# Attention B: turned probabilities as one fp32 copy, and an fp32 product with fp32 values

## The reference

```
q = (resid @ Wq) in 32 heads of 16, with rotary embedding
k, v = (resid @ Wk), (resid @ Wv) in 8 heads of 16; k with rotary embedding
att = einsum('bhgqd,bhkd->bhgqk', q, k) / sqrt(16), causal mask
probs = softmax(att)
ctx = einsum('bhgqk,bhkd->bhgqd', probs, v)
out = ctx @ Wo
```

## Time and profile before

| | us |
|---|---|
| median of 3 runs | 1158.74 (1157.28 to 1158.85) |
| the profiled execution | 1155.95 |
| its span, first to last instruction | 1154.1 |
| mean PE clock granted, share of full | 0.982 |

### The profile page before, as it was taken

The page is one execution under the profiler, slowest core; times in us unless marked ns, Lnnn a source line. Parts: engine busy times, 40 slices in busy tenths (PEclk is TensorE's granted clock), DMA queues, the critical chain, the costliest instruction groups (busy, mean ns, idle before and its releaser), DMA issues.

```text
span 1154.1 us, 25383 instructions
## 1 busy us (share of the span) xinstructions
PE 1019.4 (88%) x8608; PEld 631.0 (55%) x8608; DVE 902.5 (78%) x2021; ACT 706.9 (61%) x1561; POOL 683.6 (59%) x808
## 2 busy tenths in 40 slices
PE   1688999999999999999999978798777777777898
PEld 1345555555555555555555534455466666666554
DVE  5777877877778877877778876787779999999755
ACT  2157666666656666656666553346778888888331
POOL 3678786777678767867776514465445555555211
PEclk9999999999999999999999999899989999999999
DMA  7065354735744753555566350000000000000001
GB/s 275 16 178 142 109 139 122 170 80 137 179 118 80 191 122 74 170 142 139 108 128 156 92 127 11 1 1 1 1 1 2 0 0 0 0 0 0 1 1 73
DMA packets 180268, 94.94 MB, mean 82 GB/s; under 512 B 168288, under 2 KB 169056, under 8 KB 175584
## 3 DMA queue, kind: packets, MB, share of 16 engines
q1 hardware_dynamic: 170832, 50.85, 20.8%
q10 hardware_dynamic: 9360, 43.01, 11.4%
HBM read 49.64 MB, written 2.26 MB: 45 GB/s over the span
## 4 chain that ended last, share of the span: by engine, by line
PE 70%; ACT 11%; DVE 7%; issue 5%; POOL 3%; DMA 2%; SPq 0%; ACTq 0%; DVEq 0%; POOLq 0%
PE bank L942 14%; PE bank L944 14%; PE bank L943 14%; ACT prob L705 5%; PE bank L1273 5%; ACT ptb_hi L712 3%; PE bank L1240 3%; PE bank L1023 3%; PE bank L1024 3%; PE bank L1025 3%; PE bank L1044 3%; PE bank L1046 3%; PE bank L1045 3%; DVE xn L1364 2%; PE bank L1026 1%
## 5 line engine op out<-in xcount | busy, mean ns | idle before, releaser
L478 POOL TENSOR_TENSOR rt<-rt 128x512 f32<-128x512 f32 x80 | 101.0, 1266 | 157.6 <-DVE rt L1441 157.6
L1488 DVE SCALAR_TENSOR_TENSOR bw_hi<-bank,rden,bw_hi 128x128 f16<-128x128 f32 (+3 forms) x256 | 123.3, 544 | 60.4 <-ACT bw_hi L722 60.4
L694 ACT ACTIVATE bank<-bank,shift,c_score 128x128 f32<-128x128 f32 (+3 forms) x256 | 147.1, 604 | 2.1
L705 ACT ACTIVATE prob<-bank,shift,c_score_b 128x128 f32<-128x128 f32 (+3 forms) x256 | 137.5, 632 | 0.0
L722 ACT ACTIVATE bw_hi<-bank,rden 128x128 f16<-128x128 f32 (+3 forms) x256 | 114.0, 529 | 32.8 <-DVE rden L1481 32.8
L1455 DVE TENSOR_REDUCE smax<-bank 128x1 f32<-128x512 f32 (+3 forms) x256 | 109.3, 484 | 26.1 <-PE bank L1026 24.6
L1465 DVE TENSOR_REDUCE smax<-bank 128x1 f32<-128x128 f32 (+3 forms) x256 | 113.4, 485 | 18.7 <-PE bank L1245 16.4
L1240 PE MATMUL bank<-kt_b,qt_b 128*128 (+4 forms) x256 | 72.1, 308 | 53.7 <-ACT prob L705 53.5
L689 ACT ACTIVATE shift<-smax,c_score 128x4 f32<-128x4 f32 x64 | 19.0, 297 | 158.9 <-DVE smax L1455 158.9
L634 POOL TENSOR_TENSOR shift<-smax,c_score_b 128x1 f32<-128x1 f32 (+1 forms) x192 | 36.6, 191 | 110.3 <-DVE smax L1465 101.8
L942 PE MATMUL bank<-xt_hi,wq_hi 128*128 128x512 f16 x256 | 98.4, 384 | 3.4 <-DVE rt L1441 2.2
(11 more groups left out here) (217 smaller groups left out, 3227.4 us busy)
## 6 DMA issues: line engine op xcount, KB each, us to landing
qcode<-in_q_codes ACTq DMA_DIRECT2D x8, 1024.0 KB, 4.9
qscale<-scales_q ACTq DMA_DIRECT2D x7, 1024.0 KB, 7.6
ocode<-in_o_codes ACTq DMA_DIRECT2D x7, 1024.0 KB, 5.0
oscale<-scales_o ACTq DMA_DIRECT2D x7, 1024.0 KB, 8.4
kvcode<-in_k_codes ACTq DMA_DIRECT2D x8, 256.0 KB, 7.9
kvcode<-in_v_codes ACTq DMA_DIRECT2D x8, 256.0 KB, 8.3
x<-in_x SPq DMA_DIRECT2D x2, 1024.0 KB, 7.1
out<-x SPq DMA_DIRECT2D x8, 256.0 KB, 2.0
```

The lines of the kernel that those rows point to most:

```text
L694: act.activation(a_rows(i, s), a_rows(i, s), ACT.Exp, bias=shift[:, s % 2, c:c + 1], scale=c_score[:, 0:1], accum_out=bank[3][:, SUMS_AT + ...
L705: act.activation(prob[:, i2, S_OFF[i]:S_OFF[i] + w], bank[bk][:, o:o + w], ACT.Exp, bias=shift[:, i2, c:c + 1], scale=score[:, 0:1]).then_ ...
L1488: dve.scalar_tensor_tensor(out=p_row[:, s % 2, LO_AT[i]:LO_AT[i] + P_STEP * i + 1:P_STEP], in0=turned_back(i, s), scalar=rden[:, s % 2, c: ...
```

## The change

The halves of the turned probabilities and of the values are replaced by one fp32 tile each, `ptb` and `bv`. ACT copies pieces 0 and 2 to `ptb`, DVE piece 1; the factor 2^15 is gone; POOL has no part in it any more. `b_pv` issues one fp32 matmul where `three` stood, ten in place of thirty. DVE's `bv_lo` is gone and ACT writes the values as fp32. Turning row tile 0 now waits for ACT's copies of the step before, where it waited for DVE.

```
@@ -262,8 +262,7 @@
-        bv_hi = sb("bv_hi", [P, NT, KV_HEADS * B_VD], F16)
-        bv_lo = sb("bv_lo", [P, NT, KV_HEADS * B_VD], F16)
+        bv = sb("bv", [P, NT, KV_HEADS * B_VD], F32)
@@ -298,9 +297,7 @@
-        ptb_hi = sb("ptb_hi", [P, 2, TRI], F16)
-        ptb_lo = sb("ptb_lo", [P, 2, TRI], F16)
-        ptb_32 = sb("ptb_32", [P, 2, TRI - 2 * S], F32)
+        ptb = sb("ptb", [P, 2, TRI], F32)
@@ -349,13 +346,12 @@
...
@@ -594,9 +590,8 @@
             pool.memset(kt_b[:].rearrange("p h f n -> p (h f n)").bitcast(F32), 0.0).then_inc(zeros_done, 1)
-            for v, value in ((bv_hi, 1.0), (bv_lo, 0.0)):
-                pool.memset(v[:].rearrange("p t (h d) -> p t h d", d=B_VD)[:, :, :, B_HD:B_VD], value
-                            ).then_inc(zeros_done, 1)
+            pool.memset(bv[:].rearrange("p t (h d) -> p t h d", d=B_VD)[:, :, :, B_HD:B_VD], 1.0
+                        ).then_inc(zeros_done, 1)
@@ -616,16 +611,6 @@
-            def b_last_piece(n, i2):
...
-                piece = slice(2 * S, TRI)
-                pool.wait_ge(bpt, 3 * n + 1)
-                pool.tensor_tensor(ptb_hi[:, i2, piece], ptb_32[:, i2],
-                                   one[:].broadcast_to([P, TRI - 2 * S]), ALU.mult).then_inc(bpthi_last, 1)
-                pool.wait_ge(bpthi_last, n + 1)
-                pool.tensor_tensor(ptb_lo[:, i2, piece], ptb_32[:, i2], ptb_hi[:, i2, piece], ALU.subtract
-                                   ).then_inc(bpt_last, 1)
@@ -633,13 +618,10 @@
                                            c_score_b[:, 1:2].broadcast_to([P, c1 - c0]), ALU.mult).then_inc(bshift, 1)
-                    if not (first and s == 0):
-                        b_last_piece(n - 1, (s - 1) % 2)
...
                 b_group(j, False)
-            b_last_piece(8 * KV_HEADS - 1, 1)
@@ -705,12 +687,12 @@
-            def pt_high(base, piece, ps, done, scale, pt, banks):
...
-                w = S if piece < 2 else 2 * P
-                act.wait_ge(ps, base + piece + 1)
-                act.activation(pt[:, piece * S:piece * S + w], bank[banks[piece]][:, 0:w], ACT.Copy,
-                               scale=scale).then_inc(done, 1)
+            def b_turned(n, i2, piece):
...
+                w = S if piece < 2 else TRI - 2 * S
+                act.wait_ge(bpt_ps, 3 * n + piece + 1)
+                act.activation(ptb[:, i2, piece * S:piece * S + w], bank[B_PT_BANK[i2][piece]][:, 0:w], ACT.Copy
+                               ).then_inc(bpt_act, 1)
@@ -876,8 +858,8 @@
                 act.wait_ge(bkv_ps, t + 1)
-                act.activation(heads_v(bv_hi, t), bank[5 + t % 2][:, P:2 * P].rearrange("p (h d) -> p h d", d=B_HD),
-                               ACT.Copy, scale=PROJ_DN_B).then_inc(bv_hi_done, 1)
+                act.activation(heads_v(bv, t), bank[5 + t % 2][:, P:2 * P].rearrange("p (h d) -> p h d", d=B_HD),
+                               ACT.Copy, scale=PROJ_DN_B).then_inc(bv_done, 1)
@@ -893,7 +875,7 @@
                 if t == 0:
-                    act.wait_ge(zeros_done, 3)
+                    act.wait_ge(zeros_done, 2)
@@ -920,16 +902,15 @@
                     if not (first and s == 0):
-                        for piece in range(2):
-                            pt_high(3 * (n - 1), piece, bpt_ps, bpthi, P_UP, ptb_hi[:, (s - 1) % 2],
-                                    B_PT_BANK[(s - 1) % 2])
+                        for piece in (0, 2):
+                            b_turned(n - 1, (s - 1) % 2, piece)
...
                 b_group(j, False)
-            for piece in range(2):
-                pt_high(3 * (8 * KV_HEADS - 1), piece, bpt_ps, bpthi, P_UP, ptb_hi[:, 1], B_PT_BANK[1])
+            for piece in (0, 2):
+                b_turned(8 * KV_HEADS - 1, 1, piece)
@@ -1219,7 +1200,7 @@
                 if t >= 2:
-                    pe.wait_ge(bv_lo_done, t - 1)
+                    pe.wait_ge(bv_done, t - 1)
@@ -1256,13 +1237,13 @@
             pe.wait_ge(bt_act, 3 * NT)
-            pe.wait_ge(bv_lo_done, NT)
+            pe.wait_ge(bv_done, NT)
...
                 if i == 0 and not first:
-                    pe.wait_ge(bpt, 3 * n - 1)
+                    pe.wait_ge(bpt_act, 2 * n)
@@ -1280,16 +1261,15 @@
                     pe.wait_ge(bctx, n)
-                pe.wait_ge(bpt, 3 * n + 3)
-                pe.wait_ge(bpt_last, n + 1)
+                pe.wait_ge(bpt_act, 2 * n + 2)
+                pe.wait_ge(bpt_dve, n + 1)
                 vc = bass.ds(j * B_VD, B_VD)
-                hi, lo = ptb_hi[:, s % 2], ptb_lo[:, s % 2]
...
                         tc = slice(T_OFF[kt] + (i - kt) * P, T_OFF[kt] + (i - kt + 1) * P)
-                        vh, vl = bv_hi[:, b * ST + kt, vc], bv_lo[:, b * ST + kt, vc]
-                        mm = three(o_ap, hi[:, tc], lo[:, tc], vh, vl, kt, i + 1)
+                        mm = pe.matmul(o_ap, ptb[:, s % 2, tc], bv[:, b * ST + kt, vc], start=(kt == 0),
+                                       stop=(kt == i))
@@ -1464,13 +1444,6 @@
-            def pt_low(count, piece, hi_done, done, scale, hi, lo, banks):
-                w = S if piece < 2 else 2 * P
-                c = slice(piece * S, piece * S + w)
-                dve.wait_ge(hi_done, count)
-                dve.scalar_tensor_tensor(out=lo[:, c], in0=bank[banks[piece]][:, 0:w], scalar=scale, in1=hi[:, c],
-                                         op0=ALU.mult, op1=ALU.subtract).then_inc(done, 1)
@@ -1735,11 +1708,6 @@
                                   ALU.subtract).then_inc(bk_lo, 1)
-                dve.wait_ge(bv_hi_done, t + 1)
-                dve.scalar_tensor_tensor(out=heads_v(bv_lo, t),
-                                         in0=bank[5 + t % 2][:, P:2 * P].rearrange("p (h d) -> p h d", d=B_HD),
-                                         scalar=PROJ_DN_B, in1=heads_v(bv_hi, t), op0=ALU.mult,
-                                         op1=ALU.subtract).then_inc(bv_lo_done, 1)
@@ -1791,17 +1759,10 @@
-            def b_low_piece(n, i2, piece):
-                pt_low(2 * n + piece + 1, piece, bpthi, bpt, P_UP, ptb_hi[:, i2], ptb_lo[:, i2], B_PT_BANK[i2])
...
-            def b_low(n, i2, first):
...
-                if not first:
-                    dve.wait_ge(bpt_last, n - 1)
-                dve.wait_ge(bpt_ps, 3 * n + 3)
-                dve.tensor_scalar(ptb_32[:, i2], bank[B_PT_BANK[i2][2]][:, 0:TRI - 2 * S], P_UP, None, ALU.mult
-                                  ).then_inc(bpt, 1)
-                b_low_piece(n, i2, 0)
+            def b_turned(n, i2):
...
+                dve.wait_ge(bpt_ps, 3 * n + 2)
+                dve.tensor_copy(ptb[:, i2, S:2 * S], bank[B_PT_BANK[i2][1]][:]).then_inc(bpt_dve, 1)
@@ -1810,11 +1771,9 @@
                     if not (first and s < 1):
-                        b_low(n - 1, (s - 1) % 2, first and s < 3)
+                        b_turned(n - 1, (s - 1) % 2)
...
                         b_rden(n - 2, s % 2, first and s < 4)
-                    if not (first and s < 1):
-                        b_low_piece(n - 1, (s - 1) % 2, 1)
@@ -1824,8 +1783,7 @@
             last = 8 * KV_HEADS - 1
-            b_low(last, 1, False)
-            b_low_piece(last, 1, 1)
+            b_turned(last, 1)
```

More of the change, by code:

```diff
@@ L350, in build @@
                              "mt_ps", "mthi_done", "mt_done", "y_ps", "y_added"))
-        bq_ps, bkv_ps, bq_mul, bk_mul, bq_rot, bk_rot, bq_hi, bk_hi, bv_hi_done, bq_lo, bk_lo, bv_lo_done = (
+        bq_ps, bkv_ps, bq_mul, bk_mul, bq_rot, bk_rot, bq_hi, bk_hi, bv_done, bq_lo, bk_lo = (
             sem(n) for n in ("bq_ps", "bkv_ps", "bq_mul", "bk_mul", "bq_rot", "bk_rot", "bq_hi", "bk_hi",
-                             "bv_hi_done", "bq_lo", "bk_lo", "bv_lo_done"))
+                             "bv_done", "bq_lo", "bk_lo"))
         zeros_done, bt_ps, bt_act, bt_dve = (sem(n) for n in ("zeros_done", "bt_ps", "bt_act", "bt_dve"))
-        bs_ps, bsmax, bshift, bexp, brden, bpt_ps, bpthi, bpt, bpthi_last, bpt_last, bctx_ps, bctx = (sem(n) for n in (
-            "bs_ps", "bsmax", "bshift", "bexp", "brden", "bpt_ps", "bpthi", "bpt",
-            "bpthi_last", "bpt_last", "bctx_ps", "bctx"))
+        bs_ps, bsmax, bshift, bexp, brden, bpt_ps, bpt_act, bpt_dve, bctx_ps, bctx = (sem(n) for n in (
+            "bs_ps", "bsmax", "bshift", "bexp", "brden", "bpt_ps", "bpt_act", "bpt_dve", "bctx_ps", "bctx"))
         def load_codes(eng, n, j):
```

## The result

The changed kernel takes 1186.13 us (median of 4 runs, 1185.4 to 1187.78) against 1158.45 us (1157.28 to 1158.85) for the kernel before on the same chip: ratio 1.0243, 95% interval 1.0225 to 1.026, or 27.7 us more where 13.8 less was forecast. The profiled execution took 1185.75 us, with a span of 1183.9. One of ten executions of the kernel with the old division of the pieces took 1556.65 us at a mean granted clock of 0.659, against 0.98 in the others, and is left out of its time.

A forecast was written before the change was run, and what follows sets the result against it. It took a loop of ACT and PE, 3.54 us a head, to bound the kernel. Steps -13.4, projections -1.4, first heads +1.0 and end 0 gave -13.8 us: 1144.9 us from 1158.74, range 1138 to 1200.

The forecast's parts named there:

- the term of PE's product: PE, `b_pv`: two pairs of load and matmul a product at 70 ns each, ten products 1.40 us.
- rival B: PE, `b_pv`: four pairs a product, 220 to 280 ns, step 4.09 to 4.69 us, about 1193 to 1230 us; chance 0.20.
- rival E: PE clock falls to the 1.2 GHz level: steps 4.6 us and more, 1220 us and up; chance 0.04.
- rival C: PE product: two pairs of 83 to 111 ns, load not overlapping the matmul before; 1158 to 1193 us; chance 0.10.
- Room on PE: PE, first product matmul to next scores: 1.65 us, or 1.43 with the shortened step, hiding products up to 143 ns each.
- ACT's copies: Attention B, ACT: 256 columns fewer save 0.22 us a step, 3.54 to 3.32; 61 steps give -13.4 us.
- DVE and POOL: Attention B: DVE loses 1.09 us a step, POOL two operations; neither in the chain, so worth nothing.
- Projections: `bv_lo` leaves DVE ahead of the rotary products: seven times 0.20, 1.4 us less.
- the ring: Projections: DVE's rotary products, POOL's sum, ACT's copies and DVE's norm wait for each other; if another arm takes over, nothing saved.
- First heads: First heads of attention B at low clock: PE paces, one product falls in at double price, +1.0 us.
- The end: Last product 0.65 us longer, a DVE L1472 ahead of the reciprocal gives 0.67; zero.

The follow-up runs named there:

- the old division of the pieces: Against the kernel with single fp16 values and one pass: ACT copies pieces 0 and 1, DVE piece 2; 1154.91 us, 0.9969 of the kernel before.
- runs with 17, 64 and 128 columns: Changed kernel itself (17 moving columns in each fp32 product), and widened to 64 or 128: 1186.13, 1185.79 and 1190.57 us.
- the run with turns made as products: Against the kernel with single fp16 values and one pass: transposes replaced by fp32 matmuls with the identity; 1208.7 us against 1140.03.
- runs with four, seven and ten products: Changed kernel with six or three of its ten fp32 products left out, or none: 1141.29, 1145.4 and 1186.13 us.
- one fp16 number: Changed kernel with turned probabilities and values kept as fp16, low halves left out, multiplied in one pass: 1140.03 us, 0.9854 of the kernel before.
- The mixed kernel: Against the kernel before: four products (piece 1) fp32, six as three fp16 passes, ACT copies piece 2 as fp32, POOL splits it; 1145.75 us, 0.9894.

## Why the prediction was wrong

**The step that failed is the term of PE's product**: "A pair costs the fp16 distance plus the longer load, 25 + 45 = 70 ns". The number of pairs, two a product, was right (1280 matmuls, 20 a head), which rules out rival B; the clock of 1.00 in the steady steps rules out rival E. The pair takes 110 ns. Ten products are 2.19 us, not 1.40, against a room of 1.43. The size is that of rival C, which I gave a chance of 0.10: 83 to 111 ns a pair, step up to 4.11, up to 1193 us; measured 4.08 and 1186.

C's reason did not come true with its size. It said that a load cannot overlap the short matmul before it. But matmuls of 128 columns leave the distance at 114 ns, so load and matmul do overlap. And the forecast's reason for two pairs (one matmul carries both parts of the moving number) is not shown by the right count.

Two errors made the 70. First, the price of a pair stood in the nearest row: the turns start 111 ns apart. I took that for 128 columns at two cycles each and expected 17 columns to be cheaper. The runs with 17, 64 and 128 columns have 110, 112 and 114 ns: the price does not shrink with the columns. Second, I built the price from the lengths of two load records, and a record's length is not its occupancy: a turn's load lasts 141 ns and a product's 192, yet both pairs start 110 to 111 ns apart. (That the kind of matmul makes the load's record longer, not the data, is shown by the run with turns made as products.) Where the trace has no such pair back to back, the honest price was the whole interval between 25 and 111 ns, which put the threshold of 71.5 ns a pair in its middle and not 1.5 ns beside the forecast.

**Room on PE.** Right. The formula 3.54 + 2.19 - 1.65 = 4.08 gives the measured step. The runs with four, seven and ten products lie below, at and above the threshold, at 3.42 (mean), 3.40 and 4.08 us.

**ACT's copies.** Right in mechanism and near in size, but covered up by PE: 377 ns for the 256 columns against 376 expected, and 0.19 to 0.20 us a step where the product leaves it free (four products, one fp16 number), against 0.22. The division of the pieces alone is worth 1.2% by the ratios, 13 to 14 us.

**DVE and POOL.** Right for the steady steps: worth nothing there by themselves (old division, 3.63 against 3.61 us). Not quite right for the first heads of the kernel before, where the chain has 1.6 us of DVE in it (row maximum, L1802 and L1472, in the chain before):

```profile
847.54 0.69 DVE smax L1465
848.23 0.33 DVE ptb L1802
848.56 0.61 DVE ptb_lo L1472
```

**Projections.** Half of the 1.4 us: from the first rotary product of the queries to the last lie 46.7 us before (779.8 to 826.5) and 46.0 after (780.0 to 826.0). The mixed kernel, with `bv_lo` back, has 46.9 again (780.2 to 827.1), so the half that came is that instruction's. The other half did not come; another arm of the ring probably takes over, which no run tests.

**First heads.** The sign was wrong. In the stretches shown with the result the clock is at full from 843 us on, where the kernel before has 0.50 of it until 847.5, in the first stretch below. No product falls into the low clock any more: the first one starts at 844.74 us, when the clock is already at full. So it is not the fp32 product that brings the clock up earlier. The other runs agree. The kernel with one fp16 number has no fp32 product and is at 1.00 from 843 us on; the mixed kernel has four a head and is at 0.50 until 847.5. What does bring it up is not shown; the two kernels with the late rise are those in which DVE and POOL still make halves. The lines are from the kernel before, the changed kernel (two), the one with one fp16 number and the mixed one.

```profile
835.00:847.50 12.50, 8.65 (x46) 6.10 (x45) 6.15 (x15) 8.76 (x17) 2.81 (x10) 0.50 0.00 1
```
```profile
842.20:844.60 2.40, 1.75 (x17) 1.60 (x18) 2.21 (x5) 1.98 (x5) 0.43 (x3) 1.00 0.00 0
```
```profile
844.74 0.68 PE L1271 MATMUL bank<-bv,ptb 128*128 128x17 f32 x5
```
```profile
843.00:851.00 8.00, 5.54 (x73) 4.65 (x71) 6.26 (x16) 6.99 (x16) 1.53 (x8) 1.00 0.00 0
```
```profile
835.00:847.50 12.50, 8.62 (x42) 6.27 (x43) 6.37 (x14) 8.37 (x16) 2.77 (x10) 0.50 0.00 0
```

The earlier rise is why it is +25.5 us between the first and the last exponential, and not 61 x 0.46 = 28 (0.46 is 4.07 less the mean of 3.61).

**The end.** Forecast zero, measured 4.9 us from the last exponential on. The forecast counted one product there. The chain now holds two, of heads 62 and 63:

```profile
1096.71 2.15 PE bank L1271 x20
...
1099.45 2.68 PE bank L1271 x20
```

In the kernel before, the product of head 62 lay beside DVE's copies and off the chain. The clock adds to it: it falls to 0.78 and 0.84 in the changed kernel (first two lines), where the kernel before has 1.00 in both stretches. The run with 64 columns, whose PE does nearly the same work and waits the same 0.60 us for the context ahead of its last product, keeps 1.00 (last two lines), and takes 86.5 us from its last exponential on. That puts about half of the 4.9 us on the products (86.5 - 84.1 = 2.4) and half on the clock (89.0 - 86.5 = 2.5), an estimate from single executions.

```profile
1097.00:1105.00 8.00, 6.84 (x47) 6.06 (x47) 2.25 (x7) 1.49 (x4) 0.00 (x0) 0.78 0.01 2
1105.00:1115.00 10.00, 10.00 (x45) 4.72 (x44) 5.03 (x11) 1.19 (x2) 1.10 (x2) 0.84 0.00 0
```
```profile
1098.00:1108.00 10.00, 8.42 (x72) 7.58 (x71) 3.20 (x9) 2.96 (x6) 0.00 (x0) 1.00 0.01 2
1108.00:1118.00 10.00, 10.00 (x54) 5.37 (x53) 6.72 (x15) 1.79 (x3) 1.20 (x3) 1.00 0.00 0
```

The rule of the Trainium skill that spoke against the change is in "FP8 and Floating Point Precision", TensorE Precision Notes: four passes for true FP32. The trace has two pairs for a product, not four; whether one pair makes two passes inside it no run here shows, since the price hardly moves with the columns. The other page of the Trainium skill, "TensorE: Matmul & The Clock Gate", weight-path perf modes, says that FP32 gets no fast weight load. It is the one that bears on the outcome: 110 ns a pair against 25 agree with it.

## What to carry to other kernels

An fp32 product with few moving columns is priced by its pairs of load and matmul, not by its columns: here two pairs of 110 ns against three of 25 ns for three fp16 passes, 0.22 against 0.075 us, so it pays only in room that PE already has (four of ten products fitted, and that kernel is 1.1% faster). Before an edit that trades copies for matmuls, measure the room of the engine that receives the cost and compare it with both ends of the new price; if the threshold lies inside, the forecast has two signs. Read that price from starts of the nearest row, not from differences of record lengths. And when several engines look nearly full, move work off the one in the chain first: ACT's 256 columns were worth 1.2%, the whole relief of DVE and POOL 0.3%.

## What was not expected of the hardware

- A turn and a true product with the same operands differ on PE: one pair with a load of 141 ns against two with loads of 192 ns (fp32, 128 x 128).
- With fp32 weights the moving columns are nearly free up to 128: 110, 112 and 114 ns a pair for 17, 64 and 128.
- After the last head the clock fell in the changed kernel (0.78 and 0.84) and not in the one with 64 columns (1.00 and 1.00), although PE waits 0.60 us for the context in both. It also fell after the ACT-paced heads of the kernel with one fp16 number (0.66 from 1054 to 1064 us). So neither which engine sets the pace nor that wait tells when it falls.
